# Operands laid out on the host, expert records split on chip, and a new stage order, in a conditional feed-forward with low-rank experts

## The reference, cut to what matters

```python
h  = x @ wi.T + 2 * (x @ c_wi_a.T) @ c_wi_b.T + 2 * (x @ e_wi_a[id].T) @ e_wi_b[id].T
h  = relu(h)
y  = h @ wo.T + 2 * (h @ c_wo_a.T) @ c_wo_b.T + 2 * (h @ e_wo_a[id].T) @ e_wo_b[id].T
out = x + y
```

## Time and profile before

| | |
|---|---|
| median of 3 runs | 134.09 us (134.01 to 134.15) |
| span of the profiled execution | 132.4 us |
| its own time | not listed apart from the span; 1.7 us lie between this span and the median |
| TensorE busy | 125.6 us (95%), 826 matmuls |
| weight loads | 115.2 us (87%) |
| VectorE, ScalarE, GpSimd busy | 58.4, 49.0, 15.0 us |
| moved by DMA | 11.41 MB, mean 86 GB/s |

### The profile page before, as it was taken

How to read it: one execution, slowest core, us unless ns; L and a number is a source line. 1 busy time by engine, 2 the same in 40 slices (tenths; PEclk the granted TensorE clock), 3 DMA queues, 4 the chain that set the end, 5 groups by cost and what they waited for, 6 DMA issues and landing times.

```text
span 132.4 us, 2493 instructions
## 1 busy us (share of the span) xinstructions
PE 125.6 (95%) x826; PEld 115.2 (87%) x826; DVE 58.4 (44%) x102; ACT 49.0 (37%) x103; POOL 15.0 (11%) x47
## 2 busy tenths in 40 slices
PE   6999769999999999999999999999999999999981
PEld 6778569899999988889999988899999888899970
DVE  0174988676715364443062454450424544430232
ACT  4386828666342123333151323340413233321120
POOL 7031813004010120000010300000101000000000
PEclk9999999999999999999999999999999999999999
DMA  4759973020073522502201315004011200000112
GB/s 115 266 163 285 326 198 127 0 79 19 16 317 82 160 58 73 147 0 79 79 0 40 94 53 160 0 24 135 0 40 51 83 14 0 0 0 0 40 45 79
DMA packets 9994, 11.41 MB, mean 86 GB/s; under 512 B 2626, under 2 KB 7890, under 8 KB 9986
## 3 DMA queue, kind: packets, MB, share of 16 engines
q1 hardware_dynamic: 9010, 9.48, 24.2%
q10 hardware_dynamic: 976, 1.84, 3.7%
HBM read 7.90 MB, written 3.41 MB: 85 GB/s over the span
## 4 chain that ended last, share of the span: by engine, by line
PE 88%; DVE 4%; DMA 3%; ACT 1%; issue 1%; SPq 1%
PE bank_h L654 33%; PE bank_h L719 18%; PE bank_o L719 18%; PE bank_h L665 6%; DMA aic_nat<-in_L_cond_common_wi_a 3%; DVE bi_stack L524 3%; PE bank_x L614 2%; PE bank_x L635 2%; PE bank_x L623 2%; PE bank_o L614 2%; PE bank_h L728 2%; PE bank_o L736 1%; ACT bi_stack L440 1%; PE bank_h L736 1%; PE bank_h L614 1%
## 5 line engine op out<-in xcount | busy, mean ns | idle before, releaser
L654 PE MATMUL bank_h<-xT,wiT 128*128 128x512 f32 x192 | 49.8, 395 | 0.0
L654 PEld LDWEIGHTS bank_h<-xT,wiT 128*128 128x128 f32 x192 | 33.9, 189 | 5.7
L517 DVE SCALAR_TENSOR_TENSOR hid<-bank_h,hid 128x512 fp32r<-128x512 f32 x32 | 21.7, 689 | 23.8 <-ACT hid L458 23.8
L458 ACT ACTIVATE hid<-bank_h 128x512 fp32r<-128x512 f32 x32 | 18.8, 600 | 32.1 <-PE bank_h L665 32.1
L719 PE MATMUL bank_o<-wcat,hid 128*128 128x272 f32 x192 | 26.9, 293 | 0.0
L719 PE MATMUL bank_h<-wcat,hid 128*128 128x272 f32 x192 | 25.0, 289 | 0.0
L719 PEld LDWEIGHTS bank_o<-wcat,hid 128*128 128x128 f32 x192 | 24.6, 189 | 0.0
L719 PEld LDWEIGHTS bank_h<-wcat,hid 128*128 128x128 f32 x192 | 24.5, 188 | 0.0
L665 PEld LDWEIGHTS bank_h<-low_stack,bi_stack 128*128 128x128 f32 x64 | 11.3, 188 | 3.8 <-issue 1.7
L665 PE MATMUL bank_h<-low_stack,bi_stack 128*128 128x256 f32 x64 | 12.2, 283 | 1.5 <-DVE bi_stack L524 1.5
L517 DVE SCALAR_TENSOR_TENSOR lo_stack<-bank_h,lo_stack 16x128 fp32r<-16x128 f32 x16 | 4.5, 284 | 19.5 <-ACT lo_stack L468 19.3
(11 more groups left out here) (84 smaller groups left out, 102.1 us busy)
## 6 DMA issues: line engine op xcount, KB each, us to landing
out<-o_sb SPq DMA_DIRECT2D x16, 128.0 KB, 1.7
x_nat<-in_x SPq DMA_DIRECT2D x7, 256.0 KB, 2.8
bi_stack<-bi_parts SPq DMA_DIRECT2D x24, 64.0 KB, 2.3
wo_nat<-in_L_cond_wo SPq DMA_DIRECT2D x1, 1024.0 KB, 7.5
bi_parts<-biT ACTq DMA_DIRECT2D x2, 512.0 KB, 3.3
wi_nat<-in_L_cond_wi ACTq DMA_DIRECT2D x2, 256.0 KB, 4.0
wi_nat<-in_L_cond_wi SPq DMA_DIRECT2D x1, 512.0 KB, 4.4
ao_nat<-in_L_cond_experts_wo_a SPq DMA_DIRECT2D x1, 512.0 KB, 8.5
```

Source lines behind the costliest of these rows:

```text
L458: nc.scalar.activation(hid[HI][:, m, :], bank_h[m % 4][:, :], ACT.Relu).then_inc(hid_hi, 1)
L517: return nc.vector.scalar_tensor_tensor(out=out_, in0=src, scalar=0.0 if scale is None else scale, in1=hi.bitcast(F32), op0=op, op1=ALU.su ...
L654: nc.tensor.matmul(bank_h[m % 4][:, :], wiT[sw][:, k, f], xT[sx][:, k, :], start=(i == 0), stop=False)
```

## The change

It is a rewrite; its parts are these.

1. **Layout.** The host hands in x transposed (`x_t`) and natural (`x_n`), wi and wo transposed in four pieces, and per expert one record each of `wi_a` and `wo_a` (`rec_a`, 128 partitions × 192), of `wi_b` with the common rows, repeated four times (`rec_b`, 128 × 1024, 512 KB), and of `wo_b` (`rec_bo`, 96 × 256). All transposes of operands, both DRAM tables and the write-back go away. The common `wo` factors come as one block (`common`, three copies).
2. **Records.** SP reads the ids and gathers each sequence's records into one of two buffers. HI and LO are split from them in each step: `a` and `bo` on GpSimd, `b` HI on ScalarE, `b` LO on VectorE (step 0) or GpSimd (steps 1 to 3). x is split from SBUF by ScalarE and VectorE.
3. **Order.** No loops: up 0, up 1, down 0, up 2, down 1, up 3, down 2, down 3, with two sets of xT, hid, low and rank buffers. In up 0 the first two tiles run together, so that each 128 rows of x and wi are used as they come.
4. **Second layer.** `wo` gets its common product in up 1 (`wo_product`, eight matmuls). For the last sequence a wo of its own is made during down 2 and at the start of down 3 (`own_wo_product`, eight matmuls, with ScalarE and VectorE splits), so that its two tiles have 256 columns and need no turn and no fin. The last add and store are done in two halves, the second from ScalarE's queue.
5. **Ranks of the second layer.** ScalarE scales and copies them, VectorE splits them before the turn, and the turn is a plain matmul with a rounded identity into the same bank. ScalarE alone copies the result.
6. **Warm-up.** Eight products of zeros, not five.

```diff
-    WARM_UP = 5
+    WARM_UP = 8
+STAGES = [("up", 0), ("up", 1), ("down", 0), ("up", 2), ("down", 1), ("up", 3), ("down", 2), ("down", 3)]
...
+            sp.dma_start(idt[:, :], ids.rearrange("(o n) -> o n", o=1)).then_inc(ids_in, 16)
+            for k in range(KD):
+                sp.dma_start(w_raw[:, 0, k * 2 * P:(k + 1) * 2 * P], wi_0[k]).then_inc(wi0_in[k], 16)
+            sp.wait_ge(ids_in, 16)
+            for n in range(PAIR):
+                expert.append(sp.value_load(idt[0:1, n:n + 1], min_val=0, max_val=E - 1))
+                load_a(0, n)
+            load_b(0)
+            load_x(1)
...
+            split_a(0)
+            split_a(1)
+            split_common()
+            split_b_lo(1, 0)
+            split_b_lo(1, 1)
+            copy_ao(0, 0)
+            copy_ao(0, 1)
+            split_bo(0)
...
+            for k in range(KD):
+                act.dma_start(x_raw[:, k, :], x_t[0, k]).then_inc(x_in[k], 16)
+            for i in range(1, PIECES):
+                act.dma_start(w_raw[:, i, :], wi_t[i - 1]).then_inc(wi_in[i], 16)
...
+            def split_x_lo(q, k):
+                nc.vector.tensor_tensor(xT[q % 2][LO][:, k, :], x_raw[:, k, :], xT[q % 2][HI][:, k, :].bitcast(F32),
+                                        ALU.subtract).then_inc(xt_lo, 1)
...
+            def first_up():
+                up_first_pair()
+                up_main(0, 2)
+                up_main(0, 3)
+                ranks_in(0, 0)
+                ranks_in(0, 1)
+                up_main(0, 4)
+                up_main(0, 5)
+                for m in range(4):
+                    up_lora(0, m)
+                up_main(0, 6)
+                up_main(0, 7)
+                for m in range(4, MF):
+                    up_lora(0, m)
+                ranks_in(1, 0)
+                ranks_in(1, 1)
+            def second_up():
+                up_main(1, 0)
+                up_main(1, 1)
+                wo_product(0)
+                wo_product(1)
+                up_main(1, 2)
+                up_lora(1, 0)
...
+                for t in range(1, TT):
+                    down_main(q, t, FIRST_HALF)
+                    if not own_wo(q * TT + t - 1):
+                        turn(q, t - 1)
+                    if q == STEPS - 2:
+                        own_wo_product(t - 1)
+                    down_main(q, t, SECOND_HALF)
+                    if not own_wo(q * TT + t - 1):
+                        fin(q, t - 1)
...
+            first_up()
+            second_up()
+            down(0, None)
+            up(2, 0)
+            down(1, None)
+            up(3, 1)
+            down(2, None)
+            down(3, 2)
```

More of the change, by code:

```diff
@@ L48, in conditional_ffn @@
     BANK = 512
[L49 to L69 removed]
+    WARM_UP = 8
+    NO = 3
+    TURN_AT = BANK - P
+    assert T == BANK and PIECE == BANK and 4 * BLK == P and REC_A == A_COLS + MF * R and rec_b.shape[2] == F
+    B_LO, LOW_LO = BLK, 2 * BLK
+    WIN_AT, OUT_AT, RANK_AT = [0, R], [R, 0], [0, D]
+    ov = out.rearrange("b (u p) d -> b u p d", p=P)
     with ExitStack() as ctx:
@@ L165, in conditional_ffn @@
[L165 to L185, removed]
@@ L513, in _ @@
+            for what, q in STAGES:
+                if what == "down":
+                    down(q)
+                elif q == 0:
+                    first_up()
+                else:
+                    up(q)
+            act.wait_ge(added, STEPS * TT + 1)
+            act.dma_start(ov[B - 1, SEQ_TILES - 1][:, SECOND_COLS], o_sb[:, TT - 1, SECOND_COLS]).then_inc(stored[TT - 1], 16)
         @block.vector
@@ L603, in _ @@
+            for what, q in STAGES:
+                if what == "down":
+                    down(q)
+                elif q == 0:
+                    first_up()
+                else:
+                    up(q)
         @block.tensor
         def _(pe):
-            def run_group(name):
-                g = G[name]
-                for s, v in g["wait"]:
-                    pe.wait_ge(s, v)
-                if before[name]:
-                    pe.wait_ge(wt_out, OUT[before[name]])
-                for i, (dst, src) in enumerate(g["tiles"]):
-                    last = nc.tensor.matmul(dst, src, ident[0:src.shape[0], 0:src.shape[0]], is_transpose=True,
-                                            start=(i == 0), stop=(not g["products"] and i == len(g["tiles"]) - 1))
-                for i, (dst, lhsT, rhs) in enumerate(g["products"]):
-                    last = nc.tensor.matmul(dst, lhsT, rhs, start=False, stop=(i == len(g["products"]) - 1))
-                last.then_inc(wt_done, 1)
@@ L702, in main, with wo_product @@
-            def main(step, t, tiles=range(MF)):
-                b = t // SEQ_TILES
+            def wo_product(i):
+                if i == 0:
+                    pe.wait_ge(common_lo, 2)
+                if i < 2:
+                    pe.wait_ge(hid_lo, 6 + i)
+                else:
+                    pe.wait_ge(wo_sum, i - 1)
+                for jj in range(2):
+                    m = 2 * i + jj
+                    last = nc.tensor.matmul(bank_o[1 + i % 2][:, jj * D:(jj + 1) * D], common_st[:, m * P:(m + 1) * P],
+                                            common_st[:, F:], start=True, stop=True)
+                last.then_inc(prod_done, 1)
```

1111 lines of the change are left out of this document (585 added, 526 removed).

## The result

| | before | after |
|---|---|---|
| median | 134.06 us (134.01 to 134.15, 4 runs) | 119.61 us (118.57 to 120.49, 4 runs) |
| profiled execution | 132.4 us of span | 120.02 us, 118.2 of them span |
| ratio | | 0.8897, 95% interval 0.8852 to 0.8942 |

The change saves 14.45 us, 0.6 less than forecast. The new kernel's own runs lie 1.9 us apart, the old one's 0.14; but in the three later sets, with eleven runs of the old kernel each, those lie 2.1 to 2.8 us apart, so 0.14 is not the old kernel's spread.

The account below looks back on a forecast made before the run. TensorE was taken as the bound, with gaps only at the two ends. Start 4.7, clock 1.15, work 108.8 and tail 2.7 sum to 117.35 us of span; with 1.7 to the median, 119.0 us, range 117.2 to 122.0.

Parts of the forecast that it names:

- Steps 1, 6 and 7: TensorE's work sums to 108.8 us; up 1 and down stages add no wait; tail 2.7 us, beside 4.3.
- Step 2: Start: first half of x lands at 3.6, cast by 4.3, warm-up ends near 4.8; 4.7 us taken.
- Step 3: TensorE's rate at the start doubles near 7.0 us; matmuls from 4.7 lose 1.15 us, ends 0 to 2.5.
- rival C: The clock gives more or less: no loss 117.9 us, three microseconds longer at half rate 120.5; inside the forecast's own case.
- step 4: First up stage: `b` records land 10.0 to 11.2, ready 13.3 to 14.5, correction due 15.1; no stall, cover 0.6 us.
- Step 5: GpSimd's in-order queue: `common` lands near 14, done at 23.1, TensorE asks at 25.4; cover 2.3 us, no loss.
- Rival A: GpSimd and VectorE block each other on SBUF splits: 1 to 3 us lost, 121.0 us; chance 0.22.
- Rivals B and D: B: gathers at 200 GB/s, `b` late, 123.5 us, chance 0.08. D: transfers set the pace, slower than before, 0.03.
- Rival E: Change does not do what it says; the stage order removes no wait, counted as nothing; chance 0.01 for no difference.

Follow-up runs that it names:

- a_again: The changed kernel, unchanged, run once more in another set: 119.74 us (118.62 to 120.58), ratio 0.8865 (0.8815 to 0.8914).

## Why the prediction was right, point by point

| term of the sum | predicted | kernel after | read from |
|---|---|---|---|
| first up matmul | 4.7 | 4.54 | start timeline |
| lower rate at the start | 1.15 | 0 | longest up matmul |
| first up matmuls waiting for splits | 0 | 0.45 | 10.55 - 4.54 - 4 × 1.39 |
| TensorE idle for step 1's low-order half | 0 | 1.36 | waits |
| tail | 2.7 | 2.57 | 118.2 - 115.63 |
| TensorE's work | 108.8 | 109.3 | the rest |
| span | 117.35 | 118.2 | |

- **Steps 1, 6 and 7, TensorE's work and the tail**: right. A down stage with its up stage takes 26.91 of the 26.9 announced. The 0.5 more lies ahead of down 0. A turn takes 0.06, not 0.11, and an own product pair 0.29, not 0.24. The tail shrank by 4.3 - 2.57 = 1.7, forecast 1.6, and the run without an own wo shows that all of it is the own wo's.
- **Step 2, the start**: right within 0.2 us.
- **Step 3, the clock**: at the lower of its ends (0 to 2.5) in this profile, the "no loss" of rival C. The durations of the up matmuls (least, median, most, in ns) and what the weight loads of the first ones waited for:

```profile
L634 PE MATMUL bank_h<-xT,wiT x156: 388/394/470, 4.5 to 88.6; 128*128 128x512 f32 x156
```

```profile
PEld bank_h L634 <- DVE xT L493: 0.5, 2, 0.2
```

None takes over 0.47 us, where the first at the lower level take 0.77 (last section). So the 0.45 us that the first 24 lose is no lower rate: it lies where they wait for VectorE's splits of x and wi, which step 4 had put at nothing. The warm-up did bring the doubling forward: over eleven profiles of kernels with eight products the first 24 up matmuls take 5.82 to 6.76 us, in the two with five 7.15 and 7.54.
- **Step 4, the first correction**: the `b` records were there at 9.82 and 11.13, announced for 10.0 to 11.2, and nothing stalled there in the kernel after. The correction came 0.85 earlier than the 15.1. But the 0.6 us of cover is not enough in every execution: in `a_again` the second `b` record was cast only at 11.7 and the correction waited 1.0, and in three more profiles of the new order it waited 0.2 to 1.0.
- **Step 5, GpSimd's queue**: this is the step that failed, on the landing of `common`. It said that `common` lands near 14, that GpSimd is "done at 23.1", that TensorE asks at 25.4, "cover 2.3 us, so nothing". GpSimd was done at 25.94 and TensorE asked at 24.72, so the cover of 2.3 became an idle of 1.36. Of GpSimd's 25.94 - 23.1 = 2.84 us, 16.58 - 14 = 2.58 arose ahead of the cast of `common`: 1.9 because `common` itself landed at 15.9, 0.7 because the `a` splits stood ahead of it until 16.52. I had taken 322 GB/s for all 3.7 MB, and in the stretch with `a` and `common` it was 163; and I had put `a` of step 1 into the queue without a landing time (14.11). The blocking by VectorE makes 0.53 + 0.33 = 0.86 of the `a` splits. SP's wait in `load_x(1)`, also left out, was not the price: with `a` issued ahead of it nothing was gained.
- **Rival A**: its mark appeared (TensorE idle before a correction of step 1 for GpSimd) and the blocking is real in both directions, 0.34 to 0.87 on GpSimd and 0.69 to 1.45 on VectorE. The Trainium skill, "SBUF — State Buffer", section "Who interferes with whom", says that a VectorE instruction with two SBUF inputs contends with a GpSimd one that reads SBUF. This trace agrees, with the durations just given. But the blocking is the smaller part of the lateness, and VectorE's late x split at 39.44 cost nothing. Of the 1 to 3 us that A gave, at most 0.7 can be laid to it: without the 0.86, `common` would still not have been there before 15.9.
- **Rivals B and D**: TensorE's waits name no DMA, `b` of step 0 landed at 11.13 and not at B's 16.5, and 14.93 MB moved in the shorter time. But B's slower gathers did come, later and on `a` and `common`, and that is what step 5 lacked.
- **Rival E**: its sentence on the order, "I count nothing for it", was wrong as a statement of the order's worth. The middle was full either way, as I argued; but the sum used up 1 as cover for making wo, for GpSimd's queue and for the gathers, and that cover is what the order gives. The better-arranged of the two runs in the old order puts a price of about 7 us on it. My 119.0 stood because the sum had it in silently.

The span's 0.85 more than the sum is +1.36 for the idle, -1.15 for the rate, +0.45 for the splits, +0.5 of work, and -0.3 of start and tail. These are errors of both signs that partly cancel, so that the time came out within 0.6 is in part luck. The mechanism was as forecast in the middle and the tail, where TensorE's work alone sets the pace, and not in the head. No run takes the new layout alone: that the transposes and the old head are what the rest of the saving comes from is read from the chains of the two kernels.

**A version that is probably faster than both kernels**: the corrections of up 1 one tile later, 118.9 us against 119.55 in the one set that has both, and 119.03 in another set, where nothing stands beside it.

## What to carry to other kernels

For each wait on a DMA queue, ask which transfers stand behind it, and follow the whole list of a slow in-order engine with a landing time for every entry; a cover of two microseconds needs each of them. Take the rate for the landing times from transfers of the same kind, and don't expect a transfer that is issued earlier to land as much earlier while others are under way. When late data can't be made earlier, put independent TensorE work ahead of the wait: one tile and two small products were enough, and more, with the wo splits pulled forward, moved the wait to VectorE. An order that removes no wait from the old trace may still carry the new one, because it is the cover that other terms lean on.

## What the runs showed of the hardware

**The moment of the doubling moves between runs of like programs.** TensorE's timeline from 4.8 to 5.3 us in the kernel after, and below it in the one with still later corrections, which has the same sixteen warm-up records:

```profile
4.54 0.94 PE L634 MATMUL bank_h<-xT,wiT 128*128 128x512 f32 x3
```

```profile
4.50 1.20 PE L628 MATMUL bank_h<-xT,wiT 128*128 128x512 f32 x2
```

The first runs its 512-column matmuls at the higher level: its first record is 0.47 long, and the ends follow each other (0.94 - 0.47) / 2 = 0.24 us apart. The second is at the lower level, 1.20 - 0.77 = 0.43 us from one end to the next, with 0.77 for its first record, although what it needs of x and wi was split as early. The granted clock is listed as 1.00 in this stretch of both, so the column does not show this start; after the idle of the old order it does (0.64).

**GpSimd and VectorE.** A subtraction of 32 partitions × 1024 columns took 2.37 us on GpSimd and 1.22 on VectorE, so that GpSimd's chain for step 1, not its start alone, is long: 3.21 + 4.74 us for three of them and one of 256 columns.

**A busy DMA share does not tell what is moved.** In the kernel after the share is 1.04 from 9 to 12 us and 0.99 from 12 to 15, and the transfers moved 380 and 163 GB/s in these stretches.
